# A post-norm decoder layer on one NeuronCore: rotary halves swapped in PSUM, a retimed last batch, and the second gate/up part ahead of the last output projections

## The reference

```python
q, k, v = x @ Wq + bq, x @ Wk + bk, x @ Wv + bv          # 16 heads of 32
q, k = rope(q), rope(k)                                   # x * cos + swapped(x) * sin
attn = softmax(causal(q @ k.T / sqrt(32)))                # by batch and head
x = layernorm(x + (attn @ v) @ Wo + bo)
query, key = ctx @ Wq2.T + bq2, ctx @ Wk2.T + bk2         # 512 x 128, from a second input
x = layernorm(x + x @ softmax(query @ key.T).T)           # 512 x 512, by batch
x = layernorm(x + (silu(x @ Wg.T) * (x @ Wu.T)) @ Wd.T)   # hidden width 2048
```

## Time and profile before

| | |
|---|---|
| median of 3 runs | 1027.92 us (1027.11 to 1029.76) |
| the profiled execution, its own time | 1029.37 us |
| its span, first to last instruction | 1027.6 us |
| mean granted TensorE clock | 0.988 |
| PE busy | 977.9 us, 95% |
| DVE, ACT, POOL busy | 628.3, 494.0, 352.0 us |
| attention with its slots | up to about 420 us |

### The profile page before, as it was taken

One profiled execution on the slowest core, in us unless ns is written; L12 is line 12 of the kernel. 1 busy time (PEld: TensorE's weight loads), 2 busy tenths in 40 slices (PEclk: granted clock), 3 DMA queues, 4 the chain that ended last, 5 costly groups with the idle time before them and its releaser, 6 DMA issues.

```text
span 1027.6 us, 15734 instructions
## 1 busy us (share of the span) xinstructions
PE 977.9 (95%) x5416; PEld 792.2 (77%) x5416; DVE 628.3 (61%) x1341; ACT 494.0 (48%) x1078; POOL 352.0 (34%) x356
## 2 busy tenths in 40 slices
PE   7879999999998889899999999999999999999997
PEld 5657777777776667688888888888888888888886
DVE  5677787778874787655544475454476444564434
ACT  5576766777774674344432344332444422333332
POOL 2566646655864523222112141111141121131112
PEclk9998999999999999899999999999999999999999
DMA  5976666955765661262221244221244212243201
GB/s 219 245 184 157 172 180 157 247 138 145 217 165 133 185 172 55 93 227 75 88 93 62 92 164 164 71 84 63 92 169 159 92 63 77 83 178 113 93 31 42
DMA packets 45486, 134.53 MB, mean 131 GB/s; under 512 B 5472, under 2 KB 5600, under 8 KB 42720
## 3 DMA queue, kind: packets, MB, share of 16 engines
q1 hardware_dynamic: 45408, 133.52, 42.5%
HBM read 104.14 MB, written 25.17 MB: 126 GB/s over the span
## 4 chain that ended last, share of the span: by engine, by line
PE 79%; POOL 6%; DVE 5%; issue 4%; ACT 4%; DMA 2%; SPq 0%; DVEq 0%; POOLq 0%; ACTq 0%
PE pu L588 17%; PE pg L588 17%; PE pd L588 17%; PE pj L536 10%; PE pj L588 5%; PE pv L579 4%; PE ps L551 2%; ACT prob L758 2%; PE pa L564 2%; PE pb L564 2%; PE pj L594 2%; POOL raw L1194 1%; DVE prob L961 1%; POOL raw L1199 1%; POOL raw L1203 1%
## 5 line engine op out<-in xcount | busy, mean ns | idle before, releaser
L1284 POOL TENSOR_TENSOR g_lo<-gated,g_hi 128x512 fp32r<-128x512 f32 x63 | 81.3, 1290 | 429.3 <-ACT g_hi L849 429.3
L758 ACT ACTIVATE prob<-prob,nmax 128x512 f32<-128x512 f32 (+3 forms) x256 | 143.8, 562 | 109.5 <-DVE nmax L961 109.2
L961 DVE CUSTOM_DVE_ANT_0 prob<-ps,mask 128x512 f32<-128x512 f32 (+3 forms) x256 | 122.6, 484 | 80.2 <-PE ps L551 76.8
L1071 DVE TENSOR_TENSOR dn_lo<-f_raw,dn_hi 128x512 fp32r<-128x512 f32 x63 | 51.2, 812 | 114.3 <-ACT dn_hi L833 114.3
L551 PE MATMUL ps<-ks,qs 128*128 128x256 f32 (+2 forms) x256 | 106.3, 417 | 11.2 <-DVE nmax L961 8.2
L1092 DVE SCALAR_TENSOR_TENSOR half<-th,pg 128x512 f32<-128x512 f32 x63 | 43.2, 686 | 100.5 <-ACT th L840 100.5
L588 PE MATMUL pd<-dn_hi,g_hi 128*128 128x512 f32 x252 | 100.0, 397 | 0.0
L840 ACT ACTIVATE th<-pg 128x512 f32<-128x512 f32 x63 | 37.7, 598 | 127.6 <-PE pg L588 127.6
L588 PE MATMUL pd<-dn_lo,g_hi 128*128 128x512 f32 x252 | 98.4, 390 | 0.0
L588 PE MATMUL pd<-dn_hi,g_lo 128*128 128x512 f32 x252 | 98.1, 389 | 0.0
L849 ACT CAST g_hi<-gated 128x512 fp32r<-128x512 f32 x63 | 39.1, 621 | 118.8 <-DVE gated L1099 118.8
(11 more groups left out here) (198 smaller groups left out, 2237.6 us busy)
## 6 DMA issues: line engine op xcount, KB each, us to landing
f_raw<-in_w_ffn SPq DMA_DIRECT2D x64, 768.0 KB, 4.3
qs<-qk_scratch SPq DMA_DIRECT2D x64, 256.0 KB, 4.7
ks<-qk_scratch SPq DMA_DIRECT2D x60, 256.0 KB, 7.7
qk_scratch<-qk_hi SPq DMA_DIRECT2D x32, 256.0 KB, 2.0
qk_scratch<-raw SPq DMA_DIRECT2D x32, 256.0 KB, 2.0
res<-in_x SPq DMA_DIRECT2D x4, 1024.0 KB, 4.9
x_scratch<-res SPq DMA_DIRECT2D x4, 1024.0 KB, 5.4
x<-x_scratch SPq DMA_DIRECT2D x4, 1024.0 KB, 4.8
```

The source lines that it names most:

```text
L758: act.activation(prob[:, t % PROBS, 0:w], prob[:, t % PROBS, 0:w], ACT.Exp, bias=nmax[:, n % 2, i:i + 1], scale=-1.0, accum_out=rsum[:, n ...
L961: dve.tensor_tensor_reduce(prob[:, t % PROBS, 0:w], ps[:, t % 2, 0:w], mask[:, S - w:S], -D ** -0.5, 3e38, ALU.add, ALU.min, accum_out=nma ...
L1071: dve.tensor_tensor(lo, f_raw[i % NR][:, 2 * KT * P:], hi.bitcast(F32), ALU.subtract).then_inc(dnlo_done, 1)
L1284: pool.tensor_tensor(lo, gated[:], hi.bitcast(F32), ALU.subtract).then_inc(glo_done, 1)
```

## The change

Four things are changed.

1. For Q and K of groups 1 to 15 the shuffle writes the bank that the projection came from (`over[...]`), and the multiply by sin reads it there and writes `swp`. The shuffle no longer waits for the add before it (the multiply does), and the bank counts as emptied when sin is done. Banks are now set by kind (`pj_bank`), and K starts one slot later.
2. `LAST` begins at slot 171: V 12 to 15 take 3 slots each and come earlier, the context units ("c" to "u") start 5 to 12 slots earlier, and "c" 0 and 1 go to two banks. The context's load is at slot 191 (196 before), its split at 196 (202), and c_lo for batch 0 is made by DVE. In the last batch x1 is stored, and the residual loaded and added, at 44, 48 and 56 (40, 45, 52).
3. The first gate/up is at slot 258, between the last transposes and the last weighted product; step 1's gate/up at 264, ahead of the last O projections; steps 0 and 1 have their elementwise parts around it, on ACT, DVE and POOL.
4. Buffers are laid out anew: `e` lies over `c_hi` and `c_lo`.

```diff
-LOAD_CONTEXT, SPLIT_CONTEXT, LOAD_X1, LOAD_F = 196, 202, 211, 241
-FIRST_GU, FIRST_HIDDEN, FIRST_DN, FIRST_STEP = 257, 262, 266, 267
-LAST = [(("q", 14), 195, (3, 3, 3, 3), 0), (("r", 11), 199, (4,), 1), (("k", 14), 200, (4, 4, 4), 0),
...
+LOAD_CONTEXT, SPLIT_CONTEXT, LOAD_X1, LOAD_F = 191, 196, 192, 241
+STORE_X1, LOAD_RES, RESIDUAL = (40, 40, 40, 44), (45, 45, 45, 48), (52, 52, 52, 56)
+FIRST_GU, FIRST_HIDDEN, FIRST_GATE, NEXT_HIDDEN, FIRST_DN = 257, 258, 262, 264, 266
+LAST = [(("v", 12), 171, (4, 4, 4), 0), (("v", 13), 174, (4, 4, 4), 1), (("v", 14), 177, (4, 4, 4), 0),
...
+def pj_bank(key, start):
+    return {"q": 0, "k": 1, "r": 1, "b": 0}.get(key[0], start % TILES // 12)
...
-        out.append((("k", n), TILES * n - 24, (4, 4, 4)))
+        out.append((("k", n), TILES * n - (23 if n else 24), (4, 4, 4)))
...
+        if kind in "qk" and n:
+            eng.wait_ge(sin_done, 2 * n + "qk".index(kind) + 1)
+            return
...
             if t == LOAD_X1:
-                full(sp, ("k", GROUPS - 1))
+                full(sp, ("k", GROUPS - 3))
...
-            if t == FIRST_HIDDEN:
-                hidden(0, 0)
-                hidden(0, 1)
+            for i, at in enumerate((FIRST_HIDDEN, NEXT_HIDDEN)):
+                if t == at:
+                    hidden(i, 0)
+                    hidden(i, 1)
...
             if t == FIRST_DN:
                 dn_half(0)
-            if t == FIRST_STEP:
-                step(0)
-        for i in range(1, STEPS):
+                product(0)
+                dn_half(1)
+                gate(1)
+                product(1)
+        dn_half(2)
+        for i in range(2, STEPS):
             step(i)
...
         def swap(n, u):
             dve.wait_ge(raw_done[u], n + 1)
-            if n or u:
-                dve.wait_ge(rot_done, 2 * n + u)
-            dve.stream_shuffle(swp[:], raw[:, u, :], SWAP).then_inc(swap_done, 1)
+            if n == 0 and u:
+                dve.wait_ge(rot_done, 1)
+            dve.stream_shuffle(over[PLACE["qk"[u], n][0]] if n else swp[:], raw[:, u, :], SWAP).then_inc(swap_done, 1)
+
+        def times_sin(n, u):
+            if n:
+                dve.wait_ge(rot_done, 2 * n + u)
             dve.wait_ge(swap_done, 2 * n + u + 1)
-            dve.tensor_tensor(swp[:], swp[:], sin[:], ALU.mult).then_inc(sin_done, 1)
+            dve.tensor_tensor(swp[:], over[PLACE["qk"[u], n][0]] if n else swp[:], sin[:], ALU.mult).then_inc(sin_done, 1)
...
+            if t == SPLIT_CONTEXT + 1:
+                dve.wait_ge(chi_done, 1)
+                dve.tensor_tensor(c_lo[:].rearrange("p k s -> p (k s)"), c_raw[:].rearrange("p k s -> p (k s)"),
+                                  c_hi[:].rearrange("p k s -> p (k s)").bitcast(F32), ALU.subtract).then_inc(clo_done, 1)
```

More of the change, by code:

```diff
@@ L95, in units @@
     out = sorted([unit for unit in out if unit[0] not in late], key=lambda unit: unit[1])
-    return [unit + (n % 2,) for n, unit in enumerate(out)] + LAST
+    return [unit + (pj_bank(unit[0], unit[1]),) for unit in out] + LAST
 UNITS = units()
@@ L154, in program @@
     p_raw, p_hi, p_lo = sb("p_raw", [P, 2, CT, DK]), sb("p_hi", [P, 2, CT, DK], F32R), sb("p_lo", [P, 2, CT, DK], F32R)
-    c_raw, c_hi, c_lo = sb("c_raw", [P, CT, S]), sb("c_hi", [P, CT, S], F32R), sb("c_lo", [P, CT, S], F32R)
+    c_raw = sb("c_raw", [P, CT, S])
+    with ExitStack() as short:
+        c_hi, c_lo = sb("c_hi", [P, CT, S], F32R, short), sb("c_lo", [P, CT, S], F32R, short)
     cqk = c_raw
-    x, e = sb("x12", [P, ST, E]), sb("e", [P, KT, S])
+    e, x = sb("e", [P, KT, S]), sb("x12", [P, ST, E])
     x1T_hi, x1T_lo = sb("x1T_hi", [P, KT, S], F32R), sb("x1T_lo", [P, KT, S], F32R)
     att_hi, att_lo = sb("att_hi", [P, KT, S], F32R), sb("att_lo", [P, KT, S], F32R)
-    sb("unused1", [P, 512])
+    sb("unused1", [P, 512 + 2048])
     cqk_hi, cqk_lo = sb("cqk_hi", [P, 2, S], F32R), sb("cqk_lo", [P, 2, S], F32R)
@@ L391, in _ @@
                 load_x(KT * (b + 1) + LOAD_X.index(at))
-            if t >= 0 and b < B and at == 45:
+            if t >= 0 and b < B and at == LOAD_RES[b]:
                 if b:
@@ L410, in _ @@
                 weights(1)
-            if 0 < b < B and at == 40:
+            if 0 < b < B and at == STORE_X1[b]:
                 sp.wait_ge(x1_done, ST * b)
@@ L697, in _ @@
         for i in range(1, STEPS - 2):
-            hidden(i, 0)
-            hidden(i, 1)
+            if i > 1:
+                hidden(i, 0)
+                hidden(i, 1)
             if i // HT < B - 1:
@@ L833, in dn_half, with gate @@
             act.copy(down_halves(i)[0], f_raw[i % NR][:, 2 * KT * P:]).then_inc(dnhi_done, 1)
-        def step(i):
-            b, j = divmod(i, HT)
+        def gate(i):
             act.wait_ge(g_full, i + 1)
@@ L842, in step, with product @@
                 gu_half(i + 1)
+        def product(i):
+            b, j = divmod(i, HT)
             if j == HT - 1 and b < B - 1:
@@ L852, in step @@
                     beside(b + 1, kind, n)
+        def step(i):
+            gate(i)
+            product(i)
             if i < STEPS - 1:
@@ L906, in _ @@
                 gu_half(0)
+            if t == FIRST_GATE:
+                gate(0)
             if t == FIRST_DN:
                 dn_half(0)
-            if t == FIRST_STEP:
-                step(0)
-        for i in range(1, STEPS):
+                product(0)
[4 more added lines that the diff above has]
+        for i in range(2, STEPS):
             step(i)
@@ L1174, in _ @@
                     normalized(0, 0, x, n)
-            if t == FIRST_GU + 3:
+            if t == SPLIT_CONTEXT + 1:
+                dve.wait_ge(chi_done, 1)
+                dve.tensor_tensor(c_lo[:].rearrange("p k s -> p (k s)"), c_raw[:].rearrange("p k s -> p (k s)"),
+                                  c_hi[:].rearrange("p k s -> p (k s)").bitcast(F32), ALU.subtract).then_inc(clo_done, 1)
+            if t == FIRST_GU + 1:
                 gu_half(0)
+            if t == FIRST_GATE:
+                product(0)
             if t == FIRST_DN:
                 dn_half(0)
-            if t == FIRST_STEP:
-                step(0)
-        for i in range(1, STEPS):
+                dn_half(1)
+                product(1)
+        dn_half(2)
+        for i in range(2, STEPS):
             step(i)
@@ L1314, in _ @@
                     split_w(n, k)
-            if t >= 0 and b < B and at == 52:
+            if t >= 0 and b < B and at == RESIDUAL[b]:
                 residual(b)
@@ L1323, in _ @@
                     root(0, 0, n)
-            if t == FIRST_STEP:
+            if t == FIRST_DN + 1:
                 step(0)
-        for i in range(1, STEPS):
+                step(1)
+        for i in range(2, STEPS):
             step(i)
```

1 line of the change is left out of this document (removed), and 20 rows, old and new, of the table LAST.

## The result

The change makes the kernel slower: 1050.95 us median of 4 runs (1049.14 to 1052.04) against 1027.51 (1025.59 to 1029.76), a ratio of 1.0225 (95% interval 1.02 to 1.0251). 1014.2 had been forecast, and 1022 was the upper end of the range. The page after, the answer to the earlier trace rows: busy times, and the slices of PE and of its clock.

The account below looks back on a forecast made before the run. PE, busy 95% of the span, was taken as the bound, with only the first 440 us able to give. Halves 7.0 plus last batch 6.8 made 13.8 us of gain, hence 1014.2 us, range 1003 to 1022.

Parts of the forecast that it names:

- In the middle batches 3 or more free slots follow a Q or K in its bank, so it costs nothing: Middle batches: holding a bank until sin is done, a slot longer, was priced at nothing.
- K one slot later ... nothing: K's later start still leaves its store ahead of the stack at slot 16n-13; cost put at nothing.
- The halves themselves: Swapped halves in PSUM: shorter sin and cos multiplies cut PE's waits, 4.0 us in 100 to 300, 3.0 in 40 to 100.
- The contention that the Trainium skill states: POOL and DVE slow each other over shared SBUF interfaces; a PSUM operand should save 24 us on DVE, 7 on POOL.
- The higher fixed cost of PSUM: A 120-cycle fixed cost against 58 would add 1.9 us over 30 multiplies; set aside for the 682 ns row.
- c_lo on DVE: Last batch, first stretch: moving c_lo off POOL removes a 4.0 us wait and 1.7 us lost to the clock.
- the first stretch: Start of the last batch: 1.2 us left, including Q 15 taking bank 1 right behind K 14's sin.
- The second to fourth stretch: Last batch, energies, transposes and mixing products packed closer: 5.4, 1.0 and 4.5 us of idle left.
- such waits now take 0.4 on average and at most 0.7: Last batch, second stretch: ten units wait for a bank read two slots before, 4.0 us together.
- Rival 3: Packed energies and transposes lock PE to DVE, 16 waits 1.3 us longer, 21 us slower, 1035 us; chance 0.06.
- The end: End of attention: early gate/up parts cover waits; 2.7 us idle and 2.5 us of clock left, 5.2 in all.

Follow-up runs that it names:

- run 1: The changed kernel with ACT's copy of the reciprocals r one slot earlier, ahead of the exp of slot 16n+24; 1023.12 us, ratio 0.9951.
- run 2: The kernel before with the first part of the change alone (shuffle into the bank, banks by kind, K a slot later), old table; 1050.84 us, ratio 1.0221.
- run 3: The kernel of run 2 with the reciprocals copied one slot earlier, as in run 1; 1023.77 us, ratio 0.9953.
- run 8: The changed kernel with K one slot further back (16n-22 in place of 16n-23), the copy of the reciprocals left late; 1051.92 us, ratio 1.0235.
- run 4: The changed kernel with its first part undone (shuffle into SBUF, banks in turn, K at 16n-24), copy left late; 1034.96 us, ratio 1.0065.
- run 5: The kernel of run 3 with c_lo subtracted on DVE instead of POOL, old table of the last batch; 1018.08 us, ratio 0.9905.
- run 11: The kernel of run 1 with both gate/up parts back where they were before the change, new table kept; 1022.4 us, ratio 0.9949.
- run 7: The kernel of run 1 with the energies, transposes and mixing products pulled apart into later slots; 1029.91 us, ratio 1.0009.
- runs 6 and 10: Run 5 with both gate/up parts early, 1021.23 us; run 5 with K 14, Q 15, context projection in other banks and only the second early, 1020.9 us.

## Why the prediction was wrong

**The step that failed** is one clause: "In the middle batches 3 or more free slots follow a Q or K in its bank, so it costs nothing". For what follows it was right: in run 1 nothing between 100 and 300 us waits for sin. I looked at who follows a Q or K, and not at whom K follows. With banks by kind, K follows r, and r is emptied by an ACT copy that stands behind the exp of slot 16n+24, whose scores PE has only just issued when it comes to K at 16n+25. Its price was 27.8 us (run 1; 27.1 between runs 2 and 3), against a forecast gain of 13.8 for all. The price of the bank in the middle batches was a term put at nothing; instead PE waited 20.7 us there, and three periods at half clock came with it. The views of the trace of before could have told it: they show the copy's place on ACT, and a wait for it of 1.0 us, of an energy in the last batch that has r's bank. In the table of units r stands at 16n+23 and K at 16n+25. In the same step "K one slot later ... nothing" weighed only K's store. Beside K's bank, a slot more or less is not free (run 8).

**The halves themselves** went as forecast. Sin took 685 ns (forecast 680 to 700), cos 1283 (1290), and the shuffle 690 where I took 743. The gain on the path was put at 7.0 us. Run 3 gained 8.4 from group 0 to 11 and 6.2 from the start to group 11, by the waits that had been named, and idle in 100 to 300 us was 1.9 in run 1 where I had asked for 1.5. What I didn't count is what the old table of the last batch pays: waits for swp of 4.3 us in run 3, which leave 4.2 to 4.8 at the end (ratio 0.9953). The contention that the Trainium skill states (GPSIMD Engine Reference, Key points) is borne out: 1480 to 685 ns on DVE, 1530 to 1283 on POOL, once sin has an operand in PSUM; run 4, without the halves, keeps 1407 to 1657 ns in the middle batches. The higher fixed cost of PSUM that the Trainium skill gives (VectorE: DVE Perf Modes, the TRN2 errata) isn't seen: 685 ns against 0.69 us from SBUF alone. The row was right to go by.

**c_lo on DVE** was put at 4.0 plus 1.7 for the clock; it gave 4.9 to 5.7 in all and 4.1 in its own stretch (run 5, old table). It ran in 1668 ns rather than 1.2 us, hidden by the slots ahead of its use, as said. In the change itself the first stretch was to be left with 1.2 us, the bank that Q 15 takes behind K 14's sin included. That term was too small: this one wait took 3.3 us in the change, 3.2 in run 1 and 5.0 in run 11.

**The second to fourth stretch** were to leave 10.9 us of idle for 10.6 before, that is no gain. With the bank freed the new table takes about 4 us more there (67.8 in run 1 and 67.7 in run 11 for 63.7). The step that failed is "such waits now take 0.4 on average and at most 0.7". In the change two for att_lo took 1.6 and 1.2, and, what I hadn't listed, three for banks that ACT's exp of an energy empties took 2.2, 1.6 and 3.0. Rival 3 named the place, but with DVE as the holder, and at 21 us. Whether the packing itself or the crowded front sets this 4.5 us isn't separated: run 7 was to do it and failed.

**The end** was to be left with 5.2 us of 7.8, a gain of 2.6, and 34.5 to 31.9 is exactly that. This is luck: of idle time 1.1 us went (4.3 to 3.2), the clock cost 3.4 us as before (6.8 us at half), and the rest is in part 9 matmuls fewer. The reason was wrong too. Run 11 has the end at 31.0 with the gate/up parts where they were, and runs 6 and 10 have it at 35.6 with them moved. So it is the new table that shortens the end. Its last transposes are done 7 slots earlier, and the wait for x2T_lo falls from 1.7 to 0.6 us; whether that is all of it was not tried. With this table the early gate/up swaps a wait of 1.1 us for pT (run 11) against one of 2.3 for gu_lo (run 1).

**The sum** 13.8 = 7.0 + 6.8 would have been about 5 even with the bank freed (run 1, ratio 0.9951): the halves give 4.8, c_lo 4 to 5.7, the table takes 4.5 and the gate/up nothing. No rival had this mechanism. Rival 3, the only one slower than before, had 1035 us and 0.06.

## What to carry to other kernels

When a bank or buffer gets a new assignment, list for every user who held it last and who empties it, and look where the emptying instruction stands in its engine's queue: ready data behind a wait is not free data. Place such a copy ahead of whatever waits for the engine that will need it. Once a long wait is gone, expect the next within the same stretch, and price an edit alone before it is packed with others: here the moved gate/up gave nothing that could be measured and the new table cost 4.5 us.

## What the runs showed of the hardware beyond that

- A STREAM_SHUFFLE of 128x512 from SBUF took 690 ns into PSUM and 743 into SBUF.
- Two operands in SBUF, and POOL beside: whichever instruction started second took longer. In the trace of before the sin multiply started at 14.58 ahead of POOL's cos multiply (14.72) and took 693 ns, and cos 1703; at 46.32 it started behind cos (45.91, 1277 ns) and took 1410 itself. With one operand in PSUM both kept their lengths: at 139.85 after, sin took 684 ns inside cos (139.41, 1272 ns).
- The copy rb<-rrec on DVE took 741 ns on average after and 541 before, with the same code and shape. The traces show where the difference lies: after, 8 of the 16 copies started while one of POOL's 128x512 operations ran, and took 797 to 1586 ns, the other 8 took 426 to 429; before, 7 did, six of which took 620 to 1194, and all others 426 to 429.
- Waits of 1.9 us, once in 23 to 25 us with PE 92% busy, were followed, in three cases of the eight between 100 and 300 us, by some 3.4 us at half clock (after and run 2 alike). With waits of 0.2 in their place it stood at 1.00 there. All told the eleven waits cost a third more than they lasted: 24.7 us for 18.4. But idle time alone doesn't tell: in run 8 PE was busy for 90%, with 25 waits, nearly all of 0.5 to 1.0 us, and the clock stood at 1.00 from 100 to 300 us.
